# GNN of three attention layers on one core: a third of x1 as three rounded products, the reduced weights beside their own layer, later shift transposes moved into a pair

## The reference, cut to what matters

```python
def gat_conv(x, src, dst, W, a_src, a_dst, b):        # N=1250 nodes, D=768, H=4 heads of C=192
    h = (x @ W).reshape(N, H, C)
    as_n = (h * a_src).sum(-1)
    ad_n = (h * a_dst).sum(-1)
    e = leaky_relu(as_n[src] + ad_n[dst], 0.2)
    m = segment_max(e, dst, num_segments=N)
    p = exp(e - m[dst])
    s = segment_sum(p, dst, num_segments=N)
    alpha = p / (s[dst] + 1e-16)
    out = segment_sum(alpha[:, :, None] * h[src], dst, num_segments=N)
    return out.reshape(N, H * C) + b

# 41250 edges plus one loop for each node
x1 = relu(x @ W_ah + b_ah)
xs = [relu(gat_conv(x1, src, dst, W, a_s, a_d, b)) for W, a_s, a_d, b in three_layers]
x_out = relu(concatenate(xs, axis=1) @ W_out + b_out)
return layernorm(x + x_out)
```

## Time and profile before

| | us |
|---|---|
| median of 3 runs (lowest, highest) | 947.55 (946.79, 947.81) |
| the profiled execution | 946.64 |
| its span, first to last instruction | 945.0 |
| PE busy (share, instructions) | 921.3 (98%, 5582) |
| DVE busy | 738.9 (78%, 1067) |
| ACT busy | 372.7 (39%, 563) |
| POOL busy | 45.8 (5%, 94) |

### The profile page before, as it was taken

One profiled execution on the slowest core, in us unless ns is written; L12 is line 12 of the kernel. 1 busy time (PEld: TensorE's weight loads), 2 busy tenths in 40 slices (PEclk: granted clock), 3 DMA queues, 4 the chain that ended last, 5 costly groups with the idle time before them and its releaser, 6 DMA issues.

```text
span 945.0 us, 14231 instructions
## 1 busy us (share of the span) xinstructions
PE 921.3 (98%) x5582; PEld 866.8 (92%) x5582; DVE 738.9 (78%) x1067; ACT 372.7 (39%) x563; POOL 45.8 (5%) x94
## 2 busy tenths in 40 slices
PE   6999999999999999999999999999999999999997
PEld 2667689999999999999999999999999789999996
DVE  7999955699999799999999999998877372343232
ACT  1566333222221335554564555565555550010000
POOL 4700000000000000010010010010010100000000
PEclk9999999999999999999999999999999999999999
DMA  5350723552542821362351362249241352233111
GB/s 180 60 186 25 239 90 92 163 166 82 168 162 75 254 101 41 96 153 50 95 135 42 96 138 56 81 129 363 82 124 41 103 180 109 82 105 118 56 33 34
DMA packets 57725, 108.31 MB, mean 115 GB/s; under 512 B 14024, under 2 KB 41265, under 8 KB 56510
## 3 DMA queue, kind: packets, MB, share of 16 engines
q1 hardware_dynamic: 39212, 66.24, 22.7%
q0 software_dynamic: 5360, 18.77, 7.5%
q10 hardware_dynamic: 13090, 22.44, 7.5%
HBM read 80.34 MB, written 27.10 MB: 114 GB/s over the span
## 4 chain that ended last, share of the span: by engine, by line
PE 57%; ACT 0%; DVE 0%; issue 0%; ACTq 0%
PE ps L1416 34%; PE ps L1509 18%; PE ps L1451 2%; PE ps L1499 2%; PE ps L1496 1%; ACT R_XIN L796 0%; PE ps L1401 0%; DVE R_XIN L1203 0%; DVE stats L1193 0%; DVE R_EXP L1189 0%; DVE R_EXP L1187 0%; ACT rstd L855 0%; DVE mv L1198 0%; DVE rstd L1200 0%; ACTq L795 0%
## 5 line engine op out<-in xcount | busy, mean ns | idle before, releaser
L1416 PE MATMUL ps<-R_W 125*125 125x193 f32 x2400 | 395.7, 327 | 3.5 <-ACT R_XIN L785 2.2
L1416 PEld LDWEIGHTS ps<-R_W 125*125 125x125 f32 x2400 | 391.6, 188 | 4.7 <-ACT R_XIN L785 2.8
L770 ACT ACTIVATE R_W<-R_EXP,s 125x1250 f32<-125x1250 f32 x120 | 160.5, 1340 | 171.5 <-DVE R_EXP L1059 114.8
L1070 DVE SCALAR_TENSOR_TENSOR R_W<-R_W,R_CNT 125x1250 f32<-125x1250 f32 x120 | 174.5, 1455 | 3.3 <-DVE R_EXP L1059 2.3
L1097 DVE CUSTOM_DVE_ANT_0 R_ROWS<-R_MASK,R_ROWS 125x1250 bf16<-125x1250 bf16 x90 | 124.8, 1456 | 13.6 <-DMA R_ROWS<-as_dram 13.2
L1301 PE MATMUL ps<-Wl_hi,x_hi 128*125 128x384 f32 (+2 forms) x360 | 116.5, 342 | 0.0
L1301 PE MATMUL ps<-Wl_lo,x_hi 128*125 128x384 f32 (+2 forms) x360 | 115.8, 340 | 0.0
L1301 PE MATMUL ps<-Wl_hi,x_lo 128*125 128x384 f32 (+2 forms) x360 | 115.7, 340 | 0.0
L1509 PE MATMUL ps<-Wo_hi,xs_hi 128*125 128x384 f32 (+2 forms) x324 | 109.5, 338 | 0.3 <-PE ps L1499 0.3
L1509 PE MATMUL ps<-Wo_lo,xs_hi 128*125 128x384 f32 (+2 forms) x324 | 109.4, 338 | 0.0
L1509 PE MATMUL ps<-Wo_hi,xs_lo 128*125 128x384 f32 (+2 forms) x324 | 109.2, 337 | 0.0
(11 more groups left out here) (155 smaller groups left out, 841.5 us busy)
## 6 DMA issues: line engine op xcount, KB each, us to landing
xs_dram<-R_XIN POOLq DMA_DIRECT2D x18, 625.0 KB, 8.0
h_dram<-R_HOUT ACTq DMA_DIRECT2D x30, 336.0 KB
R_W<-h_dram SPq DMA_DIRECT2D x12, 840.0 KB
R_ROWS<-as_dram SPq DMA_DIRECT2D x12, 625.0 KB, 5.4
R_EXP<-u_dram SPq DMA_DIRECT2D x6, 1250.0 KB, 7.3
R_X<-u_dram SPq DMA_DIRECT2D x6, 1250.0 KB, 5.7
R_ROWS<-in_W_all SPq DMA_DIRECT2D x18, 384.0 KB, 3.7
Wo_sb<-in_W_out POOLq DMA_DIRECT2D x1, 6912.0 KB, 26.1
```

Source lines behind the costliest of these rows:

```text
L770: nc.scalar.activation(prob[r % PSLOTS], expo[:, r % XSLOTS], ACT.Exp, bias=s02[:, r % NT, ds(2 * p + r // NT, 1)]).then_inc(S["exp_done"], 1)
L1070: nc.vector.scalar_tensor_tensor(out=prob[r % PSLOTS], in0=prob[r % PSLOTS], scalar=HUGE, in1=cntT[:, r % NT, 0:N], op0=ALU.min, op1=ALU.m ...
L1416: ins = mm(ps[0:PT, o:o + HW], prob[(q * NT + j) % PSLOTS][:, t * PT:(t + 1) * PT], hB[:, q, j], start=(j == 0 and t % 2 == 0), stop=(j == ...
```

## The change

1. **x1.** `X1_ORDER` now takes all m of group 0, then of group 2 (250 columns), then of group 1 (500). `x1_upto` keeps 3/4 of a step for each unit up to 36 steps and then does one step for each unit. Group 1 is computed in three products of rounded operands. ScalarE rounds x of group 1 (`xg_hi`, two copies at x1_out 6 and 7) and the weights of each m (`wg_hi`, two slots, `round_wah`); VectorE makes the rests (`xg_lo`, `wg_lo`, the latter in place of the weights). TensorE waits for xg_lo and for wg_lo of its m.
2. **V beside its layer part.** Parts 0, 1 and 2 carry 8 columns each, for the four heads of layer 0, 1 and 2. There are three turns of source values instead of two (heads 0 to 3, 4 to 7, 8 to 11), and one more store to as_dram. There is a single buffer for a.
3. **VectorE's order ahead of the extra count** (`more_counts`) is new: xg_lo, the first rests of weights, layer 0 of V, rest_x1 of group 0, the other rests between blocks of layer 1, V and W of part 0; behind it the rest of layer 1 and all of layer 2.
4. **Later shifts in mid-pair.** TensorE's transposes of the second and third go move from ahead of pair 2 and 4 to r = 14 in them (banks 2 to 4 instead of 5 to 7, behind a wait for `out_evac`), ScalarE's copies from r = 10 to r = 19, and VectorE's third `shifts` from step 5 to step 9.

The diff, cut to its core (buffer places left out):

```diff
-V_TURN = 2
-V_AHEAD = V_TURN + 2
+V_TURN = 3
...
-X1_ORDER = [(m, 0) for m in range(KT)] + [(m, g) for m in range(KT) for g in (1, 2)]
+X1_ORDER = [(m, g) for g in (0, 2, 1) for m in range(KT)]
+G_AT = {0: 0, 2: KT, 1: 2 * KT}
+SLOW = 36
+SLOW_AT = 31
...
-SCORED = [2 * ROUND_A, 2 * HEADS]
+SCORED = [2 * HEADS] * LAYERS
...
-ROUND_C_AT = 5
+ROUND_C_AT = 9
+SHIFTS_AT = 14
+SHIFTS_OUT_AT = 19
...
+V0_AT = 14
+XG_AT = (6, 7)
+WG_AT = (8, 9)
+V_NEXT_AT = (8, 3)
...
-    return X1_HEAD + 3 * (u + 1) // 4
+    return min(X1_HEAD + 3 * (u + 1) // 4, SLOW) + max(0, u - SLOW_AT)
 def x1_whole(m):
-    return KT + 2 * m + 2
+    return G_AT[1] + m + 1
...
-                if l >= 2:
-                    sp.wait_ge(S["v_made"], 2 * HEADS * KT * (l - 1))
-                sp.dma_start(aB[l % 2].rearrange("p w f -> p (w f)"),
+                if l >= 1:
+                    sp.wait_ge(S["v_made"], 2 * HEADS * KT * l)
...
+            for k in range(V_HEAD, KT):
+                load_v(0, k)
+            for k in range(VSLOTS - 1):
+                load_v(1, k)
...
+            for k in range(VSLOTS - 1, V_TURN + 1):
+                load_v(1, k)
...
+            sp.wait_ge(S["turn_ps"], x1_whole(2))
+            sp.dma_start(w_raw[0], w_half(0)).then_inc(S["w_in_first"], 16)
+            for k in range(V_TURN + 1, KT):
+                load_v(1, k)
...
-            for k in range(V_AHEAD, KT):
+            for k in range(VSLOTS - 1):
+                load_v(2, k)
+            load_a(2)
+            for k in range(VSLOTS - 1, KT):
...
+                if hh >= HEADS and hh % HEADS == 0:
+                    l = hh // HEADS
+                    sp.wait_ge(S["asT_sb"], (l + 1) * len(GROUPS))
+                    sp.dma_start(as_dram[hh:hh + HEADS], asT).then_inc(S["as_stored"], 16)
+                    sp.wait_ge(S["as_stored"], 16 * (l + 2))
+                if hh == 1:
+                    sp.wait_ge(S["v_made"], 2 * HEADS * KT * LAYERS)
...
+            def round_wah(m):
+                act.wait_ge(wah_in[m], 16)
+                nc.scalar.copy(wg_hi[m % 2][:], W_ah_sb[m]).then_inc(S["wg_hi"], 1)
...
-                    load_x(i + 3 - KT)
+                    load_x(len(GROUPS) - 1 - (i + 2 - KT))
+                if i in XG_AT:
+                    kk = slice(KT // 2 * XG_AT.index(i), KT // 2 * (XG_AT.index(i) + 1))
+                    act.wait_ge(x_in[1], 16)
+                    nc.scalar.copy(xg_hi[:, kk], xT[1][:, kk]).then_inc(S["xg_hi"], 1)
+                if i in WG_AT:
+                    round_wah(WG_AT.index(i))
+                if G_AT[1] <= i < G_AT[1] + KT - 2:
+                    round_wah(i - G_AT[1] + 2)
...
+                if i == V0_AT:
+                    act.wait_ge(S["win_done"], NU)
+                    round_v(0)
...
-                    if n == 0 and t == V_LAST_AT:
-                        round_v(1)
+                    if n < LAYERS - 1 and t == V_NEXT_AT[n]:
+                        round_v(n + 1)
...
+                    if 2 <= n <= LAYERS and t == 0:
+                        act.wait_ge(S["as_stored"], 16 * n)
+                        source_rows(len(GROUPS) * (n - 1), GROUPS)
...
-                    if nth is not None and r == NT:
+                    if nth is not None and r == SHIFTS_OUT_AT:
                         act.wait_ge(S["u_stored"], 16 * (2 * nth - 1))
-                        shifts_out(nth * len(GROUPS), uT2)
+                        shifts_out(nth * len(GROUPS), uT2, 2)
...
+            def rest_wah(m):
+                dve.wait_ge(S["wg_hi"], m + 1)
+                dve.wait_ge(S["turn_ps"], G_AT[2] + m + 1)
+                nc.vector.tensor_tensor(wg_lo[m][:], W_ah_sb[m], wg_hi[m % 2][:].bitcast(f32), ALU.subtract
+                                        ).then_inc(S["wg_lo"], 1)
+            dve.wait_ge(S["xg_hi"], 2)
+            nc.vector.tensor_tensor(xg_lo[:], xT[1], xg_hi[:].bitcast(f32), ALU.subtract).then_inc(S["xg_lo"], 1)
+            rest_wah(0)
+            reduce_v(0, V_HEAD)
+            rest_wah(1)
+            for k in range(V_HEAD + 1, KT):
+                reduce_v(0, k)
             rest_x1(0, 0, KT)
-            for k in range(V_TURN - 1):
-                reduce_v(2, k)
+            for m in range(2, KT):
+                rest_wah(m)
+                if m - 2 < V_TURN:
+                    reduce_v(1, m - 2)
+            rest_v(0)
             rest_w(0)
-            rest_v(0)
-            reduce_v(2, V_TURN - 1)
+            dve.wait_ge(S["turn_ps"], x1_whole(KT - 1))
             more_counts()
             rest_x1(1, 0, KT)
             rest_x1(2, 0, KT)
             for k in range(V_TURN, KT):
-                reduce_v(2, k)
+                reduce_v(1, k)
             rest_w(1)
             rest_v(1)
+            for k in range(KT):
+                reduce_v(2, k)
...
-                    if (hh, b) == (4, 0):
+                        if REST_W_AT[hh, b] < LAYERS:
+                            rest_v(REST_W_AT[hh, b])
+                    if (hh, b) == (6, 0):
...
+                    if g == 1:
+                        pe.wait_ge(S["xg_lo"], 1)
+                        pe.wait_ge(S["wg_lo"], m + 1)
                 if i == 0 and k % (KT // G0_PARTS) == 0:
                     pe.wait_ge(x0_in[k // (KT // G0_PARTS)], 16)
-                ins = mm(bank(5 + i % 3)[:, 0:w], W_ah_sb[m][:, k], xT[g][:, k],
-                         start=(k == 0), stop=(k == KT - 1))
+                out = bank(5 + i % 3)[:, 0:w]
+                if g != 1:
+                    ins = mm(out, W_ah_sb[m][:, k], xT[g][:, k], start=(k == 0), stop=(k == KT - 1))
+                else:
+                    for n, (ww, xx) in enumerate(((wg_hi[m % 2], xg_hi), (wg_hi[m % 2], xg_lo), (wg_lo[m], xg_hi))):
+                        ins = mm(out, ww[:, k], xx[:, k], start=(k == 0 and n == 0), stop=(k == KT - 1 and n == 2))
...
+                    if 2 <= n <= LAYERS and t == 0:
+                        source_turn(n - 1, heads_of[n - 1], GROUPS)
...
+                    if nth is not None and r == SHIFTS_AT:
+                        pe.wait_ge(S["out_evac"], NT * (2 * p + 2) + 1)
+                        shifts(nth + 1, 2)
+                    if nth is not None and r == 2 * NT:
...
-            pe.wait_ge(S["attT_sb"], 9 * 2 + 1)
-            shifts(2)
             pair(2, False, nth=1)
             pair(3, False)
-            pe.wait_ge(S["attT_sb"], 9 * (PAIRS - 2) + 1)
-            shifts(3)
```

More of the change, by code:

```diff
@@ L196, in gnn_program @@
             xT.append(v)
-        W_ah_sb = []
+        W_ah_sb, W_ah_at = [], []
+        o += 4
         for m in range(KT - 1):
+            if m == 3:
+                key_t, o = view(R_W, o, KP, (CPW * WIDEST,))
+            W_ah_at.append(("R_W", o))
             v, o = view(R_W, o, KP, (KT, KP))
             W_ah_sb.append(v)
-        key_t, o = view(R_W, o, KP, (CPW * WIDEST,))
         stage, o = view(R_ROWS, 0, PT, (NT, RING), f16)
+        o += 6
         Wv, o = view(R_ROWS, o, KP, (VSLOTS, D))
         aB0, o = view(R_ROWS, o, KP, (2, D))
-        aB = [aB0, view(R_HOUT, 0, KP, (2, D))[0]]
+        W_ah_at.append(("R_ROWS", o))
         v, o = view(R_ROWS, o, KP, (KT, KP))
         W_ah_sb.append(v)
+        wide1 = GROUPS[1][1] * PT
+        xg_hi = rounded("xg_hi", "R_W", 0, (KT, wide1))
+        xg_lo = rounded("xg_lo", "R_W", KT * wide1, (KT, wide1))
+        wg_hi = [rounded(f"wg_hi{i}", "R_HOUT", D * i, (KT, KP)) for i in range(2)]
+        wg_lo = [rounded(f"wg_lo{m}", *W_ah_at[m], (KT, KP)) for m in range(KT)]
         key_j, o = view(R_ROWS, o, KP, (CPW * WIDEST,))
@@ L278, in gnn_program @@
         V = u_place[:, 0:KT * 2 * LH].rearrange("p (k h) -> p k h", k=KT)
-        heads_of = [slice(0, ROUND_A), slice(ROUND_A, LH)]
+        heads_of = [slice(HEADS * l, HEADS * (l + 1)) for l in range(LAYERS)]
         V_part = [V.rearrange("p k (w h) -> p k w h", w=2)[:, :, :, h] for h in heads_of]
@@ L318, in gnn_program @@
             more_in more_chain more_read more_ones more_ps more_stage more_mm more_mask
-            v_made v_hi v_lo x1_lo asad_sb asT_ps asT_sb as_stored
+            xg_hi xg_lo wg_hi wg_lo v_made v_hi v_lo x1_lo asad_sb asT_ps asT_sb as_stored
             max_made scores_ready b_pair_sb uT_ps uT_sb u_stored
@@ L759, in h_part @@
                     if t == U_AT and n == PARTS - 1:
-                        act.wait_ge(S["as_stored"], 48)
-                        shifts_out(0, uT)
+                        shifts_out(0, uT, 5)
             def exp_tile(p, r):
@@ L1309, in h_products, with terms @@
                 return ins
-            def hi_terms(t):
-                for i in range(2):
-                    if i == 1:
-                        pe.wait_ge(S["w_lo"], 1)
-                        pe.wait_ge(S["v_lo"], 1)
-                    for k in range(KT):
-                        h_product(0, t, k, i, False)
-            def lo_terms(t):
-                pe.wait_ge(S["x1_lo"], 1 + (t >= 4) + (t >= 8))
```

(11 more changed lines are left out.)

86 lines of the change are left out of this document (33 added, 53 removed).

## The result

The changed kernel takes **962.78 us** (median of 5, 961.60 to 963.68) against 947.55 (also of 5): the ratio is 1.0162, with a 95% interval of 1.0148 to 1.0175, so it is slower by about 15 us. The forecast was 963.8, in a range of 954 to 968. The profiled execution took 963.32, its span 961.7 (before: 946.64 and 945.0), and the mean granted clock of TensorE is 0.988 instead of 0.999.

The account below looks back on a forecast made before the run. The prediction took TensorE, busy 98% of 945.0 us, as the bound. Its terms, -5.6 + 3.9 + 1.1 - 2.1 + 17.5 + 2.0 = +16.8 on 946.64, gave 963.4; half of 0.9 more made 963.8, range 954 to 968.

Parts of the forecast that it names:

- Late u and h under W_out: Pair 4: shifts stored late, then h loads beside W_out and delays tile 20; +17.5 us, 14 to 20.
- rival (a): Pair 4: h's packets pass ahead of W_out's, so only late u counts, +5.5; 949.8 to 951.8 us, chance 0.12.
- The late u: Pair 4: u lands at 669.0, making tile 18 5.5 us late, counted within the +17.5.
- Rival (b): Pair 4: shifts reach VectorE in time if load_u is issued by about 653; 944 us, chance 0.04.
- The clock: TensorE at tile 20: idle wait loses full speed, not back at once; +2.0 us, 0 to 2.5.
- x1 products: x1 stretch: 36 steps of group 1 as three rounded products instead of plain ones; -5.6 us.
- so that holds, barely: End of the count: VectorE's last one-hot, at 88.08, comes before the count's last unit ends near 89.3.
- wg_lo wait: x1, group 1: TensorE waits for VectorE's rest of the weights at m = 2; +3.9 us, 2.5 to 5.
- rival (c): x1: no wg_lo wait, 3.9 us less, 960 us; no separate chance, included in the forecast's 0.80.
- Third turn: V: TensorE gets a third turn of ten transposes of source values; +1.1 us.
- rival (d): V2 late for part 1, or ScalarE's x rounding holds TensorE; +2 to +5, 966 to 969; beyond 968 chance 0.04.
- Shift waits: Ahead of the later shift transposes: two TensorE waits of 1.05 us go; -2.1 us.

Follow-up runs that it names:

- e2: Changed kernel, but GpSimd's load of W_out also waits until h of head 10 has landed; 951.94 us, ratio 1.0057.
- e7: Changed kernel with 60 unused identity transposes on TensorE ahead of tile 20 in pair 4; 960.19 us, ratio 1.0131.
- e6: Changed kernel with ScalarE's copies of the shifts behind exp(18) instead of exp(19); 957.30 us, ratio 1.0121.
- e5: Kernel before with only the later shifts moved to mid-pair (part 4 of the change); 961.34 us, ratio 1.0148.
- e3: Changed kernel with VectorE's rest_wah(2) ahead of rest_x1 of group 0, each later rest one reduce_v earlier; 957.88 us, ratio 1.0113.
- e4: Changed kernel with the third go of shifts back at pair 4's start and rest_wah(2) ahead of rest_x1 of group 0; 943.08 us, ratio 0.9959.
- e1: Changed kernel with only the third go of shifts (heads 10 and 11) put back at pair 4's start; 947.49 us, ratio 1.0005.

## Why the prediction was right

It was right in its place and its mechanism: h under W_out is the largest term, and e2 and e7 show it. That the total came so close, +16.8 forecast and +16.7 measured between the profiled executions, is luck: the late h was 2.9 us less than forecast, everything ahead of tile 18 gave 2.0 less than forecast, and the clock behind tile 20 cost 0.8 more.

**Late u and h under W_out: +17.5, measured +14.6** (4.6 before tile 18, 2.7 in tiles 18 and 19, 7.3 before tile 20; it begins 13.96 later than before, at 686.94, since TensorE was 0.7 ahead at tile 18). The mechanism is the one foretold: exponent(5,0) waited 12.96 (13 foretold), W_out and h went packet for packet (266 to 268 in 5 us), and e2 shows that W_out beside it is the cause. Tile 20 began 3.6 us before the foretold 690.5, for two reasons. u was in at 667.3 instead of 669.0: the step from store to load took 1.77 us, where I took 3.0 from two rows with 2.69 and 4.66 (even my lower bound was too high), and exp(19) came 0.7 earlier than the earlier trace rows. And h came 19.6 us behind u (667.3 to 686.9) instead of 21.5. The forecast let all of h's 1,250 rows pass at 55 a microsecond from 669 on, and W_out end just before h. But W_out's first packets came only near 667, 6 us after its issue. From 662 to 668 the queues moved:

```profile
q1 hardware_dynamic: 695, 1.60, 90.1%
q0 software_dynamic: 31, 0.19, 10.2%
```

Some 420 of these 695 packets are rows of h, which had a third of its way behind it. From 682 to 687, on the other hand, SP's queue passed only 40 packets a microsecond, some of them already the larger ones of the next u, and W_out was in at 693.5, after h. So rival (a), by which h's packets pass ahead of W_out's, held for a third of them. The Trainium skill (DMA: Bandwidth & Descriptors, "Queues, rings and completion order") states that each DMA engine takes turns between the queues that have work for it, a packet at a time. The trace agrees, with 266 packets of 6 KB beside 268 of 768 bytes.

**The late u is within it.** e6 took it away, and h stayed the bound. For rival (a), which counted u alone and gave 949.8 to 951.8, e2 is the case: 951.94. The rival was well priced, but its condition (h ahead of W_out) did not hold for most of h. Rival (b) needed load_u issued by about 653; it was issued at 660.53.

**The clock: +2.0, measured +2.8 behind tile 20, and 1.6 more in x1.** I had taken the loss at the start of the kernel, four matmuls behind an idle engine; here the engine had come back at half speed once before, for tiles 18 and 19 (9.28 us instead of 6.54). That this made it dearer isn't shown: e6, without such a stretch before tile 20, lost 1.7 there, but e5, with one, 2.1, and e3, with one, 2.9. Mean granted clock, from the windows (width, busy time of PE, PEld, DVE, ACT and POOL, the clock, the DMA share, GB/s):

```profile
668.00:675.00 7.00, 4.66 (x14) 4.66 (x15) 7.00 (x6) 3.12 (x3) 0.00 (x0) 0.54 1.02 373
675.00:682.00 7.00, 4.62 (x27) 4.32 (x26) 6.97 (x9) 3.65 (x4) 0.00 (x0) 0.97 1.04 368
682.00:692.00 10.00, 5.06 (x16) 5.09 (x17) 5.44 (x4) 3.14 (x10) 0.00 (x0) 0.51 1.01 376
```

The clock rose to full (2.4 GHz) near 675, when tiles 18 and 19 had run for some 5 us, and was at half (1.2 GHz) again when tile 20 came; it stayed there until about 692. e7, which filled 6.7 us of the wait, has 1.00 in all windows from 675 to 695 and loses 0.1 at most. What tiles 18 and 19 lost was swallowed by the wait for h, as foretold.

**x1 products: -5.6, measured -4.2 to -4.7.** A rounded product of 500 columns takes 0.2265 us (0.228 foretold), so 36 steps give 5.7. But I let 1.2 of it fall into the count, whose last unit should have ended at 89.3, and it ended at 90.12. VectorE's last one-hot ended at 88.64 instead of 88.08, but not by the change: it ends at 88.56 in e5, with the old front, and at 88.07 in e4, with the new one. In e4, where nothing else disturbs, the count ends 0.95 earlier (89.56 against 90.51) and what follows is 3.78 shorter; in e3 it is 0.46 and 3.79. This was the step "so that holds, barely", and it didn't quite.

**wg_lo wait: +3.9, measured +3.06 and 1.6 of clock.** VectorE's wg_lo(2) ended at 108.9 (108.3 foretold), but TensorE arrived at 106.0 and not at 104.4, about half of it because of the later count. With the late count, this wait and its clock, the first h product, foretold at 124.7, is at 126.84: the x1 half cost 0.45, where -1.7 was forecast. No wait for m = 3, 4 and 5, as said; rival (c), no wait at all, is e3's state, and fell for the changed kernel.

**A wait not foreseen: +0.66.** The extra count's first matmul (L1270 at 133.00) stood 0.66 us for VectorE, which does the weights' rests and V first and the extra count's one-hots after them. I had priced V and the rests for their own users and not for the extra count behind them on the same engine.

**Third turn: +1.1, measured 1.1,** and V2 was in time, so that rival (d) fell too: the copy of the earlier trace rows ran at 176.51, and TensorE didn't stop. **Shift waits: -2.1, measured -2.1;** none is left.

Added up in the order of the timeline: x1 with its wait and clock +0.45 at the first h product (126.84 against the last of the earlier trace rows); +1.8 when the first shift transposes start (305.94; 304.17 before), from the third turn (1.07) and the extra count (0.66), less 0.4 that I haven't traced; less the two waits (2.1), one turn of transposes that comes later now (1.07) and an untraced 0.3: -1.7 at tile 6 of pair 4 (625.49 against the earlier trace rows); that turn again, so -0.7 where tile 18 is due; +4.6 late u; +2.7 half clock in tiles 18 and 19; +7.3 late h; +2.8 clock behind it. That is 16.7 us. (Ahead of tile 18 it is -0.7, where the forecast's terms give -2.7.)

**What stays open.** Behind the same wait of 3.06 us in x1 TensorE's clock fell in the profiled executions of the changed kernel, e2 and e7, and stayed full in those of e1 and e6. In e2 and e7 six matmuls ran at full speed first and the next eight at half. Why it falls in one and not in another isn't shown. e1's twelve executions fit a chance of this kind: the four with a mean clock of 0.997 or more took 945.3 to 947.0 us, the eight with 0.995 or less 946.7 to 950.0. But the medians of the two groups are 2.5 us apart and the clock in x1 costs 1.6, so it can't be all, and only one of the twelve was profiled. In e4, which has no such wait, all five lie within 942.0 and 944.3, at 0.997 or more. The Trainium skill (TensorE: Matmul & The Clock Gate, "What's actually happening") says too, of the start of a kernel, that the number of slow matmuls differs between runs of one kernel; what decides it no run here shows.

## What to carry to other kernels

A step that is moved later takes its transfers along: look who else is released by the same store, and what stands beside it in the queues then. Here one store released u, h and the 6.9 MB of W_out. Before, h was slow under W_out as well: its load was issued at 640.50, and nearly all its rows (1,237) had passed only by 661. But nobody wanted it before 673.0. Moving the store by 30 us took this slack away. The engine that had been 98% busy lost some 17 us in pair 4 by it, and two waits of 1.05 us were saved. If a large load with long rows must run beside a small one with short rows, issue the small one first and let the large one wait for it: one wait gave back 10.8 us, while releasing both 4.3 us earlier gave 5.5 in the median.

Where a wait on TensorE is a few microseconds long, add to its price what the clock may cost behind it: here nothing to 1.6 us behind a wait of 3.06, and 1.5 to 2.9 behind waits of 4.06 to 9.57, the long ones no dearer than the short.

## What the runs showed of the hardware

**The clock behind short waits.** Behind 3.06 us of idleness in the middle of dense work the first seven matmuls ran at half speed in some executions (in the changed kernel's, above), and at full speed in others, as here in e1:

```profile
108.88 0.47 PE L1321 MATMUL ps<-xg_hi,wg_hi 128*128 128x500 f32 x1 [3.06 <-DVE wg_lo L1054]
109.19 0.39 PE L1321 MATMUL ps<-xg_lo,wg_hi 128*128 128x500 f32 x1
109.41 0.39 PE L1321 MATMUL ps<-xg_hi,wg_lo 128*128 128x500 f32 x1
```

Behind the 3.26 us before tile 20 in e7 it stayed full. Waits of 4.06 to 4.61 us (tile 18 of the changed kernel, e2, e3, e5, e7) lost it each time, and so did those of 7.31 to 9.57 before tile 20 (the changed kernel, e3, e5, e6). The Trainium skill (TensorE: Matmul & The Clock Gate, "HAM oscillation — how this bites in real kernels") tells of a kernel in which each wait for a DMA makes the next burst start slow; these runs agree for the waits of 4.06 us and more, and show the 3.06 us wait on either side.

**Packets and queues.** A load of 768-byte rows on SP's queue passed 54 to 55 packets a microsecond beside a load of 6 KB packets on the software queue, so 0.04 MB/us of the 0.37 that both moved together. h took 11.7 us from issue to landing without W_out beside it (e2), and 26 with it. The large load was slowed far less: 24.4 us where it came last (e2), 26.1 in the kernel before, 32.0 beside u and h in the changed one.
